# Batch 1's x issued from ScalarE's queue, and a factor stack filled by four one-sided transfers per copy

## What is computed

```python
# x: (32, 512, 512), factors f: (32, 1, 512, 16), cond: (32, 512), W: (512, 512), fc_bias: (512,)
z1 = einsum('bfi,bir->bfr', x, f[:, 0]) / 512
z  = einsum('bfr,bor->bfo', z1, f[:, 0]) / 16
y  = einsum('bfi,oi->bfo', x, W) + fc_bias + z + cond[:, None, :]
out = x + gelu(y, approximate=False)
```

## Time and profile before

| | us |
|---|---|
| median of 3 runs | 378.2 (377.73 to 378.36) |
| the profiled execution | 378.88 |
| its span, first to last instruction | 377.1 |
| TensorE matmul busy | 370.7 (98% of the span) |
| VectorE busy | 297.8 (79%) |
| ScalarE busy | 207.6 (55%) |

### The profile page before, as it was taken

One profiled execution on the slowest core, in us unless ns is written; L12 is line 12 of the kernel. 1 busy time (PEld: TensorE's weight loads), 2 busy tenths in 40 slices (PEclk: granted clock), 3 DMA queues, 4 the chain that ended last, 5 costly groups with the idle time before them and its releaser, 6 DMA issues.

```text
span 377.1 us, 7821 instructions
## 1 busy us (share of the span) xinstructions
PE 370.7 (98%) x3129; PEld 313.8 (83%) x3129; DVE 297.8 (79%) x185; ACT 207.6 (55%) x217; POOL 0.4 (0%) x5
## 2 busy tenths in 40 slices
PE   8989999999999999999999999999999999999995
PEld 6768888888888888888888888888888888888884
DVE  7699778977788977878978778887778977788832
ACT  5377445665456565555565546575445665445532
POOL 0000000000000000000000000000000000000000
PEclk9999999999999999999999999999999999999999
DMA  7999998777977778977778877778976778874222
GB/s 242 218 239 358 277 288 263 214 226 229 272 213 238 213 226 229 245 247 236 197 226 240 253 231 234 202 231 240 262 226 221 212 226 244 252 222 141 111 113 111
DMA packets 24796, 85.49 MB, mean 227 GB/s; under 512 B 4832, under 2 KB 5216, under 8 KB 20816
## 3 DMA queue, kind: packets, MB, share of 16 engines
q1 hardware_dynamic: 24496, 84.92, 76.3%
q10 hardware_dynamic: 288, 0.39, 0.3%
HBM read 35.75 MB, written 33.55 MB: 184 GB/s over the span
## 4 chain that ended last, share of the span: by engine, by line
PE 93%; DMA 3%; ACT 1%; SPq 1%; issue 1%; DVE 0%
PE y L495 87%; PE update L588 3%; DMA x_in<-x_t 2%; DMA x_in<-x_first 1%; PE y L479 1%; PE y L487 1%; PE y L483 1%; SPq L194 1%; ACT result L315 0%; ACT w_high L280 0%; DVE result L425 0%; ACT x_high L287 0%; SPq L206 0%; ACT f_parts L263 0%; SPq L204 0%
## 5 line engine op out<-in xcount | busy, mean ns | idle before, releaser
L495 PE MATMUL y<-x_high,w_high 64*128 64x512 f32 x960 | 190.2, 386 | 1.4 <-ACT result L315 1.4
L495 PE MATMUL y<-x_low,w_high 64*128 64x512 f32 x960 | 190.1, 386 | 0.0
L315 ACT ACTIVATE result<-y,bias 128x512 f32<-128x512 f32 x129 | 81.4, 682 | 154.2 <-PE y L495 146.4
L495 PE MATMUL y<-x_high,w_low 64*128 64x512 f32 x960 | 129.1, 386 | 0.0
L425 DVE TENSOR_TENSOR result<-result,x_in 128x1024 f32<-128x1024 f32 (+1 forms) x66 | 78.3, 1187 | 58.3 <-ACT result L315 58.3
L495 PEld LDWEIGHTS y<-x_high,w_high 64*128 64x128 f32 x960 | 93.2, 184 | 17.5 <-issue 1.8
L495 PEld LDWEIGHTS y<-x_low,w_high 64*128 64x128 f32 x960 | 93.2, 184 | 15.6
L495 PEld LDWEIGHTS y<-x_high,w_low 64*128 64x128 f32 x960 | 93.1, 184 | 15.7
L364 DVE SCALAR_TENSOR_TENSOR full_w<-update,base_w 128x2048 f32<-128x2048 f32 (+2 forms) x35 | 73.4, 2097 | 14.2 <-PE update L588 12.9
L360 DVE TENSOR_TENSOR x_low<-x_in,x_high 128x2048 fp32r<-128x2048 f32 (+1 forms) x35 | 73.5, 2100 | 2.1 <-ACT x_high L274 2.1
L360 DVE TENSOR_TENSOR w_low<-full_w,w_high 128x2048 fp32r<-128x2048 f32 (+1 forms) x35 | 73.6, 2102 | 0.3
(11 more groups left out here) (28 smaller groups left out, 31.7 us busy)
## 6 DMA issues: line engine op xcount, KB each, us to landing
out_t<-result SPq DMA_DIRECT2D x63, 512.0 KB, 3.4
x_in<-x_t SPq DMA_DIRECT2D x31, 1024.0 KB, 6.6
f_stack<-f_parts SPq DMA_DIRECT2D x122, 64.0 KB, 5.2
f_stack<-f_parts SPq DMA_DIRECT2D x61, 128.0 KB, 4.9
x_in<-x_first SPq DMA_DIRECT2D x4, 256.0 KB, 4.5
base_w<-w_t SPq DMA_DIRECT2D x3, 256.0 KB, 5.3
f_parts<-factors SPq DMA_DIRECT2D x1, 768.0 KB, 8.2
base_w<-w_t ACTq DMA_DIRECT2D x1, 256.0 KB, 2.7
```

The source lines that it names most:

```text
L315: nc.scalar.activation(result[j % SLOTS][:, m, cols], y[m][:, cols], ACT.Gelu, bias=bias[:, bass.ds(b * CHUNKS + m, 1)]).then_inc(gelu_rea ...
L495: return nc.tensor.matmul(y[m][:, :], w[rows, c, m * P:(m + 1) * P], x[rows, c, :], start=first, stop=last)
```

## The change

Two edits.

1. `load_x(0, 1)`, the 1 MB of x of batch 1, is no longer issued by SyncE behind batch 1's stack, but by ScalarE, right behind the `w_high` piece of batch 0's second chunk.
2. A copy of a stack is made by four transfers, not three. Before: 16 rows with both sides high, 16 rows with both sides low (64 KB each, 2 KB at a time), and 32 rows of shifted pairs (128 KB, 4 KB at a time). Now: each transfer fills one side of 32 rows, 64 KB in pieces of 2 KB. In rows 0 to 31 both sides are high, low alternately; in rows 32 to 63 side 0 is high, low and side 1 is low, high. The pairs are the same four, in another order of the rows, and the bytes are the same. `PART_DMAS`, by which TensorE counts the landings it waits for, goes from 3 to 4.

```diff
-    PART_DMAS = 3
+    PART_DMAS = 4
...
-            high, low = rows[:, 0:1, :], rows[:, 1:2, :]
-            shifted = bass.AP(tensor=rows.tensor, offset=rows.offset,
-                              ap=[list(rows.ap[0]), [FEATURES, 2], [1, 2 * FEATURES]])
+            high_low, low_high = rows[:, 0:2, :], rows[:, 1:3, :]
             for copy in range(1 if in_whole(t, j) else TILES):
-                for first, count, pairs in ((0, RANK, high.to_broadcast([RANK, 2, FEATURES])),
-                                            (RANK, RANK, low.to_broadcast([RANK, 2, FEATURES])),
-                                            (2 * RANK, 2 * RANK, shifted)):
+                for first, side, pair in ((0, 0, high_low), (0, 1, high_low),
+                                          (2 * RANK, 0, high_low), (2 * RANK, 1, low_high)):
                     row = copy * TILE + first
-                    engine.dma_start(f_stack[slot][row:row + count, :, :].bitcast(fp32),
-                                     pairs).then_inc(stacked[slot], 16)
+                    engine.dma_start(f_stack[slot][row:row + 2 * RANK, side, :].bitcast(fp32),
+                                     pair).then_inc(stacked[slot], 16)
...
             stack_factors(sp, 0, 1)
-            load_x(sp, 0, 1)
             sp.dma_start(f_parts[:, 1, 2, :], factors[1]).then_inc(f_loaded[1], 16)
...
+                if c == 1:
+                    load_x(act, 0, 1)
```

## The result

| us | before | changed |
|---|---|---|
| median of 6 runs | 378.35 (377.73 to 378.71) | 383.95 (379.75 to 385.68) |
| the profiled execution, its span | 378.88, 377.1 | 384.17, 382.4 |
| mean granted clock in the profiled execution | 1.0 | 0.989 |

The ratio is 1.0132, with a 95% interval from 1.0081 to 1.0183. The forecast was 377.7 and its range ended at 379.2, so it was wrong, and on the wrong side. The spread is as telling as the median: one of the six executions took 379.75 us at a clock of 1.0, the five others 383.67 to 385.68 at 0.99. Before, six executions lay within 1 us.

A forecast was written before the change was run, and what follows sets the result against it. TensorE bounds the kernel from 22.18 us on; before that, batch 1's x does. Earlier x wins 1.7 us, the stack wait loses 1.2: 0.5 won, median 378.2 - 0.5 = 377.7 us, range 376.5 to 379.2.

The forecast's parts named there:

- what bounds the kernel: TensorE alone from 22.18 us on; before that, the chain from batch 1's x, landing at 17.14, can be shortened.
- The gain from x's earlier landing: Start of batch 1 on TensorE: 20.5 instead of 22.18 us if x lands before 15.5, 1.7 us won.
- the stack's form and the extra issues: Stack copies: 2 KB pieces change no rate; two more issues per batch, 1.3 us of SyncE, are hidden by its waits.
- the wait for batch 1's stack: TensorE in mid batch 0: stack lands at 14.5 behind x's block, 1.2 us lost, bounds 0 and 1.9.
- rival C: Before batch 1's rank update: a lagging DMA engine delays the stack to 16.3, TensorE waits 3.0 us; 379.5 us, chance 0.16.
- the 0.7 us that I let x give back: Batch 1's stack landing: x's block of 2.7 us delays it less, 0.3 from filling the dip, the rest from overlap.
- how two queues share: DMA engines, batch 1's x and stack: an engine serves x in one 2.7 us block, ahead of most of the stack.
- the rival of the smallest chance: Rival D, batch 1's start: x still lands at about 17, the stack on time; 378.2 us (377.8 to 378.6), chance 0.12.
- The term put at nothing without a reason: the clock: TensorE's granted clock after a stop: the prediction names no such term, in its sum or in any rival.

The follow-up runs named there:

- after_again: The changed kernel, unchanged, measured once more on another occasion and chip; 382.11 us, ratio 1.007 to the kernel before; its profiled execution took 378.88 us.
- fillers: Changed kernel plus 18 useless matmuls on TensorE, some 4.1 us, in front of the wait for batch 1's stack; 381.63 us, ratio 1.0082 to the kernel before.
- e3_x_late: Changed kernel, but ScalarE issues x of batch 1 one chunk later, behind the third chunk's `w_high`; 378.24 us, ratio 1.0001 to the kernel before.
- In quarters: Changed kernel, but ScalarE issues x of batch 1 as four transfers of 32 partitions; 381.8 us, ratio 1.0075 to the kernel before.

## Why the prediction was wrong

**Read rightly: what bounds the kernel.** The loss is wholly ahead of 28 us, the pitch of 11.33 us behind it is untouched, and x's landing was what opened batch 1. The gain from x's earlier landing was there too: in `after_again` ScalarE began `x_high` at 14.13, 3 us earlier than in the earlier trace rows, and x was off the path.

**Read rightly: the stack's form and the extra issues.** Worth nothing: 1.0004 (0.999 to 1.0017). No later rank update of the changed kernel waited for its stack.

**The step that failed: the wait for batch 1's stack, put at 1.2 us and at most 1.9.** The step had the stack land at 12.5 + 2.7 - 0.7 = 14.5. In the profiled execution it landed at 18.4 and TensorE waited 5.0 us, since two DMA engines came 2.7 and 4.3 us after the others; that part is taken up under rival C. Undisturbed it landed at 15.1 and the wait was 1.67 and 1.75 us, near the upper bound of 1.9. Of the 0.7 us that I let x give back, the dip in the earlier trace rows and the overlap gave 0.1 (12.5 + 2.7 - 15.1). With that the balance is nil: start of batch 1 at 22.26 against 22.18, where I had 21.7. The forecast of 0.5 us won was this 0.7 and no more, and it was an argument without a row for its second half.

**Right in its result, wrong in its reason: how two queues share.** The earlier trace rows were read as "each queue gives a whole transfer in turn", and the Trainium skill's rule of turns (DMA: Bandwidth & Descriptors, section Queues, rings and completion order) seemed to fit. The sentence was right about the block and wrong about why. The traces show order of issue: the swapped queues (64 KB alone on ScalarE's queue behind 1 MB on SyncE's, none of it taken up before 12.0 us) speak against turns, and one queue with the same order gives the same time, 1.0029 against 1.0038. Rows 10 fit that as well: ScalarE's `base_w` and SyncE's first x piece were issued in that order. Where page and runs differ, the runs decide, for a backlog like the one here. The Trainium skill's other rule (same page, section Issuing engines are not separate DMA queues), that issuing from a second engine saves only the time of issuing, fits these traces, and I had put it with the rival of the smallest chance: an issue 1.6 us earlier (8.41 for 9.97) is all that ScalarE's queue gave x, and with it x took its place from three of the stack's four transfers.

**The rival that decided: C, with both its terms too small.** I had the mechanism, an engine that lags with x's block in front of its part of the stack, and gave it 0.16. Even so its time, 379.5, was far from the median of 383.95. It took two engines, 4.3 us behind at the worst instead of the 1.8 that one trace of before showed, and a wait of 5.0 us instead of 3.0. I took the size of a laggard from a single execution in which nothing important was queued behind it. In the trace of before the laggard delays x only, and what shows of it is at most the 1.43 us for which TensorE stood still before batch 1; after the change it delays the operand on which TensorE stands in the middle of batch 0. The kernel became more sensitive to something that the trace of before already had.

**The term put at nothing without a reason: the clock.** It was 2.1 us for a hole of 4.6 us. The trace of before shows a clock of 1.00 throughout, with one hole of 1.4 us, and I never asked what a longer one does; no rival's sum has it either.

The sum for the profiled execution: TensorE could have started batch 1 at 20.5; 0.15 for batch 0, which ran that much later (13.46 for 13.31), 5.0 for the wait and 2.1 for the clock make 27.75. Measured: 27.57. Against 22.18 that is 5.4 us, and the profiled times differ by 384.17 - 378.88 = 5.3.

## What to carry to other kernels

In a backlog like this one, moving a transfer to another queue moved it forward in one common order and everything issued after it back; so write down that order by the times at which issues end, and put the small transfer with the tight consumer first. A wait of an in-order engine for a DMA should be priced with the slowest DMA engine of several executions, not with the median or with one trace. And a stop of TensorE has two prices, the stop and the clock behind it: waits up to 1.75 us were free here, those of 3.1 to 5.0 us cost 1.7 to 2.9 us more.

## What the runs showed of the hardware

- Two queues kept one common order. Where two issues overlap, their ends seem to decide: with fillers the stack's first issue began at 8.21 and x's at 8.50, but x's took 0.36 us and the stack's 0.69, so x's ended 0.04 us ahead; and there the first transfer of the stack was down only at 13.9, together with x's block. In `after_again` (7.85 with 0.69, 8.40 with 0.33) the stack's ended first, and it was down at 10.6. In `e3_x_late` the factors' issue began at 10.89 (0.59) and x's at 11.06 (0.36), so x's ended 0.06 us ahead, and x was down first, its first mark at 16.27 against 16.55. These are three traces and the swapped queues do not speak against it; that the ends and not the starts decide is what they suggest, not more.
- Interleaving gained no overlap in the one trace that has it. In quarters, x and the stack's pieces together moved 256 + 64 KB per 1.2 to 1.45 us and were done at 17.0 and 16.4, against 14.1 and 15.1 with x in one piece.
- Issues into a full backlog were slow on ScalarE's queue too: 2.88 us for three, with a compute engine's stream behind them.
- In some executions some DMA engines fell 3 to 4 us behind within the first 18 us, and the share of such executions was 5 of 6, 6 of 10 and 2 of 12 in three measurements. Nothing in these runs shows the cause.
- After waits of 3.10, 3.53 and 5.01 us the granted clock was at 0.50 for 3.4, 5.9 and 4.0 us of work; after 1.67 and 1.75 us it stayed at 1.00.
